# The first units of a fused two-layer kernel's last stage, in another order

## The chip, the cores and the metric

The kernel runs on one core of one Trainium2 chip. A core has TensorE (PE in the profile, with PEld for its weight loads), VectorE (DVE), ScalarE (ACT), GpSimd (POOL) and SyncE (SP), which here only issues transfers. Each engine works through its own instruction stream in order and waits for the others by semaphores. The metric is device time in microseconds (us) of one execution; lower is better.

## The reference, cut to what matters

The input is x, 8 rows of 1024 tokens with 256 features, in float32. Two layers follow each other, each adding a product to x. The last stage of the kernel computes the second one:

```python
xn = _layernorm(x)                                     # first layer
q, k, v = split(xn @ W); q = elu(q) + 1; k = elu(k) + 1
s = (q @ (k.T @ v)) / (q @ k.sum(tokens) + 1e-6)       # per row of x
e = argmax(xn @ gate_w.T)                              # one of 8 experts per token
x = x + s * silu((relu(xn @ wg[e])**2 * (xn @ wu[e])) @ wd[e])
xn = _layernorm(x)                                     # second layer
q, k, v = split(xn @ W_qkv)
scores = where(causal, q @ k.T * scale, -inf)          # in blocks of 128 tokens
p = exp(scores - max(scores)); p = p / (sum(p) + 1e-6)
s = (p @ v) @ W_out.T + b_out
x = x + s * silu(_layernorm(xn) * ln_g + ln_b)
```

The second gate of the reference also has a routed attention, which picks 8 // 16 = 0 tokens for these shapes and so adds nothing.

## The kernel before, in words

The program has three stages: `first_layer`, `experts` and `second_layer`. The tokens are 64 tiles of 128, handled as 32 units of two tiles. `z.res` holds all 64 tiles on the chip, from first to last. At the end of the first layer a tile of `z.res` holds the query rows. They become the attention's values by a product with the key-value matrix of their row of x ("values"). For the last 8 units of that work, `END`, this is done at the beginning of `second_layer`. TensorE multiplies (`whole_values`, L189), VectorE inverts the row sums (`invert_sums`, L195 and L197), and ScalarE scales into `z.res` (`scale_values`, L203). Two bank pairs, `s2_ps` and `pa_ps`, take turns, so `values(p)` waits until ScalarE has emptied its pair of two products ago.

Also there, TensorE folds the second layer's weights (`fold(0)` makes the query-key matrix in `t_ps`, `fold(1)` the value-output matrix in `v_ps`, L1561 and L1566). ScalarE copies the results to `wqk` and `wvo` (L1671). `clear` (L1570) writes constants to banks that later matmuls add to.

The experts' rows were stored to `expert_dram`, sorted by expert. For a unit, GpSimd gathers them with two indirect transfers into one of 4 slots of `four` (L1857). VectorE multiplies the unit's values with them (`scale_rows`, L1695), and x is added. For units 0 to 7 (`DIRECT`) SyncE loads x into a buffer (L1460) and VectorE adds it (`sum_x`, L1701); for the others a GpSimd transfer adds it in `z.res` (`add_x`, L1867). The layer norm then goes through VectorE statistics (L1713, L1723, L1729 to L1731), a GpSimd power and product (`norm_scale`, L1875 and L1877) and a ScalarE apply (`norm_apply`, L1626).

The unit then passes TensorE: `turn` (L1501), `q` (L1488), `v` (L1510), `scores` (L1530), `turn_probs` (L1520) and `attend` (L1541). ScalarE copies and exponentiates in between. VectorE finds the maximum (L1756), prepares the gate (L1737, L1744, L1750), applies it (`gate_rows`, L1778) and adds the rest (`result`, L1784). SyncE stores (L1465).

Each engine runs a `step(n, ...)` for each n. The steps until n = 7 are written out, 8 to 23 are in a loop of eight, and the rest is written out again. In a step the engines handle different units: TensorE has `q(n)` and `turn(n + 1)`, ScalarE has `norm_apply(n + 2)`, VectorE has `result(n - 2)` first, then the statistics of n + 3 between the gate's parts, and `scale_rows(n + 6)` last. GpSimd has `norm_scale(n + 2)`, `add_x(n + 5)` and `gather(n + 8)`; `add_x` and what follows it wait for `scale_rows(n + 5)`.

At the beginning of the stage, TensorE's order is values of END[0], fold 0, fold 1, values of END[1], then the six others, then three clears. VectorE puts `step(-6)` (scale, sum and norm of unit 0) behind the inversions of END[3] and `step(-5)` (unit 1) behind those of END[5]. GpSimd gathers units 0, 1 and 2 before it computes the norm scale of unit 0.

## Time and profile before

| what | us |
| --- | --- |
| median of 3 runs without a profile | 550.27 (549.64 to 550.29) |
| the profiled execution, whole | 555.51 |
| its span, first to last instruction | 553.9 |
| TensorE busy in the span | 508.8 (92%) |
| VectorE busy | 453.5 (82%) |
| ScalarE busy | 391.8 (71%) |
| GpSimd busy | 323.4 (58%) |
| mean granted TensorE clock | 0.987 of full |

The rows are from the one profiled execution, whose whole time is 5.24 us above the median of the runs without a profile. Times in the rows are microseconds from the start of its span. The last stage begins near 328 us and ends with the span. Busy shares are averages over three stages with different limits, so the stage itself has to be read.

### The profile page before, as it was taken

The page shows a single profiled execution, that of the slowest core. Times are in us where ns is not written, and L with a number is a line of the kernel's source. Part 1 is how long each engine was busy: PE and PEld are TensorE (multiplying, and loading weights), DVE is VectorE, ACT ScalarE, POOL GpSimd, SP SyncE. Part 2 cuts the span into 40 slices and gives each one's busy share as a digit, 9 for nine tenths or more (in the row PEclk, how much of TensorE's full clock was granted, in tenths as well). Part 3 has the DMA queues.
Part 4 walks back from the last instruction along what each step waited for, and adds up shares of the span by engine and source line. Part 5 has one row for each costly group of instructions (what it writes and reads, how often), then busy time and mean ns, then how long its engine had stood idle before and what let it go on. Part 6 is the DMA issues. An engine that isn't in the chain of part 4 may idle for free.

```text
span 553.9 us, 12747 instructions
## 1 busy us (share of the span) xinstructions
PE 508.8 (92%) x3554; PEld 468.5 (85%) x3555; DVE 453.5 (82%) x1467; ACT 391.8 (71%) x891; POOL 323.4 (58%) x403
## 2 busy tenths in 40 slices
PE   1899999999999898698899998889999999999995
PEld 0899999999999897498899987668888888888884
DVE  4698888899977665558878774799999999999985
ACT  3687777778777853366677764567888888888884
POOL 4458887878767646222122105876888888787400
PEclk9999999999999999899999999899999999999998
DMA  8833233232311004546677746134655665565311
GB/s 230 219 94 115 83 109 107 85 103 86 105 49 40 30 31 142 125 113 192 196 242 224 228 138 207 57 110 91 139 140 115 128 138 134 114 135 131 78 59 57
DMA packets 59548, 68.07 MB, mean 123 GB/s; under 512 B 11880, under 2 KB 53744, under 8 KB 59504
## 3 DMA queue, kind: packets, MB, share of 16 engines
q1 hardware_dynamic: 45104, 39.73, 23.9%
q0 software_dynamic: 14400, 27.80, 20.8%
q8 instruction: 21, 0.34, 0.3%
q14 instruction: 23, 0.19, 0.1%
HBM read 40.25 MB, written 27.26 MB: 122 GB/s over the span
## 4 chain that ended last, share of the span: by engine, by line
PE 36%; DVE 32%; issue 14%; POOL 7%; ACT 6%; DMA 2%; DVEq 1%; another core or an unknown queue 1%; POOLq 0%; SPq 0%; ACTq 0%
PE gu_ps L1109 5%; PE v_ps L1510 4%; PE q_ps L1488 4%; PE t_ps L1085 3%; PE y_ps L1128 3%; DVE res L696 2%; DVE stats L661 2%; POOL four L1857 2%; POOL rstd L1875 2%; PE s_ps L1530 2%; DVE kf L702 2%; DVE k L708 2%; DVE xt L689 2%; DVE zg L1737 2%; DVE att L1778 1%
## 5 line engine op out<-in xcount | busy, mean ns | idle before, releaser
L1857 POOL DMA_INDIRECT four<-expert_rows,gather_u x64 | 68.7, 1073 | 41.4 <-DMA expert_rows<-y 23.0
L950 POOL DMA_INDIRECT sorted_rows<-xn,row_u x64 | 65.0, 1016 | 15.4 <-issue 14.2
L1488 PE MATMUL q_ps<-xt,wqk 128*128 128x256 f32 x256 | 63.0, 390 | 0.8 <-ACT xt L1606 0.8
L934 POOL TENSOR_TENSOR xn<-xn 128x512 fp32r<-128x512 f32 x32 | 42.9, 1341 | 33.0 <-ACT xn L551 32.9
L1510 PE MATMUL v_ps<-wvo,xt 128*128 128x256 f32 x256 | 60.6, 379 | 0.0
L209 POOL DMA_DIRECT2D four<-sorted_rows x36 | 19.4, 540 | 67.9 <-issue 39.9
L1488 PEld LDWEIGHTS q_ps<-xt,wqk 128*128 128x128 f32 x256 | 50.3, 197 | 8.2 <-ACT xt L1606 1.0
L1875 POOL TENSOR_TENSOR rstd<-var_eps,neg_half 128x4 f32<-128x4 f32 x32 | 38.5, 1202 | 21.0 <-DVE var_eps L1731 10.3
L1510 PEld LDWEIGHTS v_ps<-wvo,xt 128*128 128x128 f32 x256 | 46.3, 190 | 5.0
L1626 ACT ACTIVATE xn2nd<-res,shift,rstd 128x256 f32<-128x256 f32 (+1 forms) x64 | 34.8, 594 | 8.6 <-POOL shift L1877 8.3
L579 ACT ACTIVATE k<-kf 128x512 fp32r<-128x512 f32 x32 | 20.2, 632 | 29.0 <-DVE kf L702 26.9
L1109 PE MATMUL gu_ps<-wgu,xgt 128*128 x288 | 40.0, 282 | 0.0
L166 PE MATMUL tq_ps<-xt,wq 128*128 128x256 f32 x128 | 38.9, 304 | 0.2 <-DVE res L696 0.2
L541 ACT ACTIVATE xn<-four,shift,rstd 128x255 f32<-128x255 f32 x64 | 34.8, 597 | 6.0 <-POOL shift L928 5.9
L166 PE MATMUL m_ps<-k,xn 128*128 128x256 f32 x128 | 36.6, 286 | 2.4 <-DVE k L708 2.4
L166 PE MATMUL k_ps<-wkg,xt 128*128 128x264 f32 x128 | 37.9, 296 | 0.0
L167 PE MATMUL k_ps<-wkg,xt 128*128 128x264 f32 x128 | 37.0, 289 | 0.0
L168 PE MATMUL k_ps<-wkg,xt 128*128 128x264 f32 x128 | 36.8, 287 | 0.0
L167 PE MATMUL tq_ps<-xt,wq 128*128 128x256 f32 x128 | 36.3, 283 | 0.0
L168 PE MATMUL tq_ps<-xt,wq 128*128 128x256 f32 x128 | 36.2, 283 | 0.0
L1109 PEld LDWEIGHTS gu_ps<-wgu,xgt 128*128 128x128 f32 x288 | 35.0, 191 | 1.2
L168 PE MATMUL m_ps<-k,xn 128*128 128x256 f32 x128 | 36.0, 282 | 0.0
(254 smaller groups left out, 1783.2 us busy)
## 6 DMA issues: line engine op xcount, KB each, us to landing
expert_rows<-y SPq DMA_DIRECT2D x36, 256.0 KB, 2.9
four<-in_L_attn_x SPq DMA_DIRECT2D x32, 256.0 KB
out_rows<-att SPq DMA_DIRECT2D x32, 256.0 KB, 2.3
res<-in_L_attn_x POOLq DMA_DIRECT2D x24, 256.0 KB
four<-sorted_rows SPq DMA_DIRECT2D x36, 128.0 KB, 2.4
four<-sorted_rows POOLq DMA_DIRECT2D x36, 128.0 KB, 2.8
wdn<-in_L_ffn_wd SPq DMA_DIRECT2D x2, 512.0 KB, 7.0
sorted_rows<-res SPq DMA_DIRECT2D x8, 128.0 KB, 5.6
```

The lines of the kernel that those rows point to most:

```text
L166: nc.tensor.matmul(out, lhs[0], rhs[0], start=first, stop=False, **kw)
L167: nc.tensor.matmul(out, lhs[0], rhs[1], start=False, stop=False, **kw)
L168: return nc.tensor.matmul(out, lhs[1], rhs[0], start=False, stop=last, **kw)
L541: m = nc.scalar.activation(xn[:, i, t, 0:D - 1], xa[:, i % X_SLOTS, t, 0:D - 1], ACT.Identity, bias=shift[:, i % X_SLOTS, t:t + 1], scale= ...
L934: nc.gpsimd.tensor_tensor(xn2[:, s, 1], xn[:, i], xn2[:, s, 0].bitcast(F32), ALU.subtract).then_inc(g["xn_split"], 1)
L950: nc.gpsimd.indirect_dma_start(out=z.sorted_dram.ap(), out_offset=bass.IndirectOffsetOnAxis(ap=row_u[:, i // CU, k:k + 1], axis=0), in_=xn ...
L1109: m = nc.tensor.matmul(gu_ps[:, i % 2, u * 2 * DE:(u + 1) * 2 * DE], xgt[:, i, k, u, :], z.wgu[:, k, bass.ds(e[u], 1), :].rearrange("p a f ...
L1488: m = nc.tensor.matmul(q_ps[:, j, :], wqk[:, k, j * P:(j + 1) * P], xt[:, i % 2, k, :], start=(j == 0 and k == 0), stop=(k == KD - 1), ski ...
L1510: m = nc.tensor.matmul(v_ps[:, t, :], xt[:, i % 2, k, t * P:(t + 1) * P], wvo[:, k, :], start=(t == 0 and k == 0), stop=(k == KD - 1), ski ...
L1626: m = nc.scalar.activation(xn[:, i % SLOTS, t, :].unsqueeze(1), one_tile(n, t), ACT.Identity, bias=shift[:, i % SLOTS, t:t + 1], scale=rst ...
L1857: nc.gpsimd.indirect_dma_start(out=moe[:, i % SLOTS, t, :], out_offset=None, in_=z.expert_dram.ap(), in_offset=bass.IndirectOffsetOnAxis(a ...
L1875: nc.gpsimd.tensor_tensor(rstd[:, i % SLOTS], var_eps[:, i % SLOTS], z.neg_half[:, 0:2 * UT].rearrange("p (a t) -> p a t", a=2), ALU.pow). ...
```

## The change

TensorE computes the values of END[0] to END[6] in a row. Then comes fold 0, then the values of END[7], and fold 1 last. The clears of `s2_ps` go ahead of the ones for `t_ps`. ScalarE follows: rows of END[0] to END[6], the copy of fold 0, the norm apply of unit 0, rows of END[7], the copy of fold 1.

VectorE handles the unit n + 3 in step n for the first eight units, scale, sum and norm together, where it had unit n + 6. Later units are scaled five ahead (`scale_rows(n + 5)`) where it was six, and the statistics, the moments and the small norm operations of unit n + 3 move behind `gate_rows`. The step of unit 0 is now behind the inversions of END[4], that of unit 1 behind END[6].

GpSimd gathers units 0 and 1 and then alternates: norm scale of 0, gather 2, norm scale of 1, gather 3, norm scale of 2, gather 4, norm scale of 3, gather 5, norm scale of 4, gathers 6 and 7, norm scale of 5, gathers 8 and 9. From step 4 on it has `add_x(n + 4)` and `gather(n + 6)`, where it had n + 5 and n + 8.

```diff
@@ tensor
             values(END[0])
+            pe.wait_ge(z.moe_sems["silu_ready"], z.SLOTS // 2)
+            for p in END[1:-1]:
+                values(p)
             fold(0, t_ps)
+            values(END[-1])
             pe.wait_ge(z.moe_sems["hid_ready"], z.SLOTS // 2)
             fold(1, v_ps)
             clear(a_one[:].rearrange("p t d -> p (t d)"))
-            pe.wait_ge(z.moe_sems["silu_ready"], z.SLOTS // 2)
-            values(END[1])
+            pe.wait_ge(z.rows_ready, UT * (UNITS - 1))
+            for o in (s2_ps[:, 0], s2_ps[:, 1]):
+                clear(o)
...
-            for p in END[2:]:
-                values(p)
+            pe.wait_ge(z.rows_ready, UT * UNITS)
+            clear(pa_ps[:, 1]).then_inc(g["banks_cleared"], 1)
             pe.wait_ge(g["folded_copied"], 2)
-            pe.wait_ge(z.rows_ready, UT * UNITS)
-
-            for o in (s2_ps[:, 0], s2_ps[:, 1], pa_ps[:, 1]):
-                m = clear(o)
-            m.then_inc(g["banks_cleared"], 1)
             run(pe, -1, step, UNITS)
@@ scalar
-            rows(END[0])
+            for p in END[:-1]:
+                rows(p)
             copy_folded(0, wqk, t_ps)
+            step(-2, TURN - 2, 0)
+            rows(END[-1])
             copy_folded(1, wvo, v_ps)
-            for p in END[1:6]:
-                rows(p)
-            step(-2, TURN - 2, 0)
-            for p in END[6:]:
-                rows(p)
@@ vector, in step
+                direct = isinstance(n, int) and n + 3 < DIRECT
                 result(n - 2, at(i, -2))
...
                 centre_gate(*next_one)
                 gate(*back)
                 base_divisor(*back)
                 scale_gate(*next_one)
+                if direct:
+                    scale_rows(*ahead)
                 maximum(n, i)
                 invert_divisor(*back)
                 gate_rows(*back)
...
+                if direct:
+                    sum_x(*ahead)
+                if isinstance(n, int) and n == DIRECT - 4:
+                    scale_rows(n + 4, at(i, 4))
+                x1_complete(*ahead)
+                if there(n + 8, TURN):
+                    index(n + 8, at(i, 8))
+                norm_stats(*ahead)
+                stats_complete(*ahead)
+                if not isinstance(n, int) or n + 5 > DIRECT:
+                    scale_rows(n + 5, at(i, 5))
+                find_moments(*ahead)
+                prepare_norm(*ahead)
@@ vector, start
-            divisors(END[0])
...
+            for p in END[:5]:
+                divisors(p)
+            step(-3, TURN - 3, 0)
             divisors(END[5])
-            step(-5, TURN - 5, 0)
             divisors(END[6])
+            step(-2, TURN - 2, 0)
             divisors(END[7])
-            run(dve, -4, step, UNITS + 1)
+            run(dve, -1, step, UNITS + 1)
@@ gpsimd
+            def load_rows(n):
+                rows_free(n, n % TURN)
+                gather(n, n % TURN)
+
+            def begin(n):
+
+                norm_scale(n + 2, n + 2)
+                if n < 2:
+                    load_rows(n + 4)
+                else:
+                    load_rows(2 * n + 2)
+                    load_rows(2 * n + 3)
+
             def step(n, i, _):
...
+                if isinstance(n, int) and n < SLOTS:
+                    begin(n)
+                    return
+                index_known(n + 6)
+                if isinstance(n, int) and n == SLOTS:
                     norm_scale(n + 2, at(i, 2))
-                if not direct:
-                    add_x(n + 5, at(i, 5))
-                gather(n + 8, at(i, 8))
+                    rows_scaled(n + 4, at(i, 4))
+                else:
+                    rows_scaled(n + 4, at(i, 4))
+                    norm_scale(n + 2, at(i, 2))
+                add_x(n + 4, at(i, 4))
+                gather(n + 6, at(i, 6))
...
-            run(pool, -8, step, UNITS - 3)
+            load_rows(0)
+            load_rows(1)
+            run(pool, -2, step, UNITS - 3)
```

## Rows read from the trace of the kernel before

**Rows 1.** The page: busy time of each engine; the last chain by engine

```profile
PE 508.8 (92%) x3554; PEld 468.5 (85%) x3555; DVE 453.5 (82%) x1467; ACT 391.8 (71%) x891; POOL 323.4 (58%) x403
...
PE 36%; DVE 32%; issue 14%; POOL 7%; ACT 6%; DMA 2%; DVEq 1%; another core or an unknown queue 1%; POOLq 0%; SPq 0%; ACTq 0%
```

**Rows 2.** Timeline of PE from 318 us: start, duration, what, idle before

```profile
328.58 1.91 PE L189 MATMUL s_ps<-kvf,res 128*128 128x258 f32 x8
330.33 1.89 PE L1561 MATMUL t_ps<-wdn 128*128 128x256 f32 x8
...
334.43 1.91 PE L189 MATMUL pa_ps<-kvf,res 128*128 128x258 f32 x8
...
344.90 1.98 PE L189 MATMUL s_ps<-kvf,res 128*128 128x258 f32 x8 [1.42 <-ACT res L203]
...
350.69 0.60 PE L1501 MATMUL t_ps<-ident,xn2nd 128*128 128x128 f32 x4
352.06 3.62 PE L1488 MATMUL q_ps<-xt,wqk 128*128 128x256 f32 x8 [0.77 <-ACT xt L1606]
```

**Rows 3.** Timeline of DVE from 318 us

```profile
330.53 0.16 DVE L195 TENSOR_SCALAR zsum<-s_ps 128x2 f32<-128x2 f32 x1 [0.43 <-PE s_ps L189]
...
340.79 0.69 DVE L1695 TENSOR_TENSOR res<-four,res 128x512 f32<-128x512 f32 x1 [0.39 <-DMA four<-expert_rows,gather_u]
...
343.46 0.16 DVE L1731 TENSOR_SCALAR var_eps<-moments 128x2 f32<-128x2 f32 x1
...
358.50 0.72 DVE L1695 TENSOR_TENSOR res<-four,res 128x512 f32<-128x512 f32 x1 [0.95 <-DMA four<-expert_rows,gather_u]
```

**Rows 4.** Timeline of DVE from 380 us: two `result` operations, one step apart

```profile
388.63 0.68 DVE L1784 TENSOR_TENSOR att<-att,res 128x512 f32<-128x512 f32 x1
...
394.60 0.69 DVE L1784 TENSOR_TENSOR att<-att,res 128x512 f32<-128x512 f32 x1
```

**Rows 5.** Timeline of ACT from 318 us

```profile
330.93 0.84 ACT L203 ACTIVATE res<-s_ps,zinv 128x256 f32<-128x256 f32 x2 [1.54 <-DVE zinv L197]
...
370.03 0.60 ACT L1598 ACTIVATE qt<-q_ps 128x512 f32<-128x512 f32 x1 [3.54 <-remote]
```

**Rows 6.** Timeline of POOL from 310 us

```profile
335.40 0.97 POOL L1857 DMA_INDIRECT four<-expert_rows,gather_u  x1 [0.30 <-issue]
...
343.77 1.04 POOL L1875 TENSOR_TENSOR rstd<-var_eps,neg_half 128x4 f32<-128x4 f32 x1 [2.39 <-DVE var_eps L1731]
344.90 0.60 POOL L1877 TENSOR_TENSOR shift<-neg_mean,rstd 128x2 f32<-128x2 f32 x1
...
355.77 0.96 POOL L1857 DMA_INDIRECT four<-expert_rows,gather_u  x1 [0.30 <-issue]
...
378.01 1.32 POOL L1867 DMA_DIRECT2D res<-in_L_attn_x  x1
```

**Rows 7.** Timeline of SP's queue from 326 us: x loads of units 4 to 7

```profile
334.41 2.52 SPq L1460 DMA_DIRECT2D wdn<-in_L_attn_x  x4
```

**Rows 8.** Windows: span, busy times, granted PE clock, DMA share, GB/s

```profile
352.06:355.48 3.42, 3.42 (x8) 2.75 (x9) 3.25 (x11) 1.23 (x3) 3.15 (x4) 0.51 0.22 67
```

**Rows 9.** Timeline of POOL from 376 us: norm scales and a gather

```profile
394.91 1.28 POOL L1875 TENSOR_TENSOR rstd<-var_eps,neg_half 128x4 f32<-128x4 f32 x1 [0.30 <-issue]
...
418.34 1.51 POOL L1857 DMA_INDIRECT four<-expert_rows,gather_u  x1 [0.31 <-issue]
...
498.52 1.31 POOL L1875 TENSOR_TENSOR rstd<-var_eps,neg_half 128x4 f32<-128x4 f32 x1
```

**Rows 10.** Timeline of PE from 472 us and from 424 us

```profile
483.44 0.66 PE L1501 MATMUL t_ps<-ident,xn2nd 128*128 128x128 f32 x4 [0.57 <-ACT xn2nd L1626]
...
535.00 1.89 PE L1488 MATMUL q_ps<-xt,wqk 128*128 128x256 f32 x8
...
540.87 1.89 PE L1488 MATMUL q_ps<-xt,wqk 128*128 128x256 f32 x8
```

**Rows 11.** DMA issues from 325 to 400 us: size, us to landing

```profile
out_rows<-att SPq DMA_DIRECT2D x5, 256.0 KB, 2.2
```

More of the change, by code:

```diff
@@ L1395, in second_layer @@
     SLOTS, TURN = 4, 8
-    DIRECT, NORMED = 2 * SLOTS, SLOTS
+    DIRECT = 2 * SLOTS
     MOE_SPACE = 3648
@@ L1784, in result @@
                     nc.vector.tensor_tensor(att[:, i % SLOTS], att[:, i % SLOTS], tiles(n), ALU.add).then_inc(g["out_ready"], 1)
-            def first_rows(n, i):
-                scale_rows(n, i)
-                sum_x(n, i)
-            def first_norm(n, i):
-                x1_complete(n, i)
-                norm_stats(n, i)
-                stats_complete(n, i)
-                find_moments(n, i)
-                prepare_norm(n, i)
             def step(n, i, _):
                 back, next_one, ahead = (n - 1, at(i, -1)), (n + 1, at(i, 1)), (n + 3, at(i, 3))
-                normed = isinstance(n, int) and n + 3 < NORMED
+                direct = isinstance(n, int) and n + 3 < DIRECT
                 result(n - 2, at(i, -2))
-                if not normed:
-                    x1_complete(*ahead)
-                if there(n + 9, TURN):
-                    index(n + 9, at(i, 9))
-                if not normed:
-                    norm_stats(*ahead)
-                    stats_complete(*ahead)
                 centre_gate(*next_one)
-                if not normed:
-                    find_moments(*ahead)
                 gate(*back)
-                if not normed:
-                    prepare_norm(*ahead)
                 base_divisor(*back)
                 scale_gate(*next_one)
+                if direct:
+                    scale_rows(*ahead)
                 maximum(n, i)
@@ L1823, in step, with index_known, rows_free @@
                     dve.wait_ge(z.rows_ready, UT * UNITS)
[L1824 to L1829 removed]
+                if direct:
[11 more added lines that the diff above has]
+                prepare_norm(*ahead)
             def divisors(p):
                 invert_sums(nc, dve, z, p, value_banks(p))
[L1834 to L1839 removed]
+            for p in END[:5]:
+                divisors(p)
+            step(-3, TURN - 3, 0)
             divisors(END[5])
[L1841 removed]
             divisors(END[6])
+            step(-2, TURN - 2, 0)
             divisors(END[7])
[L1844 removed]
+            run(dve, -1, step, UNITS + 1)
         def gpsimd(pool):
[L1847 removed]
+            def index_known(n):
                 if there(n):
                     pool.wait_ge(z.index_ready, n + 1)
[L1851 to L1852 removed]
+            def rows_free(n, i):
+                index_known(n)
+                if there(n, SLOTS):
+                    pool.wait_ge(g["moe_scaled"], n - SLOTS + 1)
             def gather(n, i):
```

23 lines of the change are left out of this document (removed).

## The prediction

> **What bounds the kernel now.** The page comes first [rows 1]. TensorE is busy for 92% of the span, VectorE for 82%, and the chain that ended last is shared between them, 36% and 32%. So neither can be dropped as a bound, and the stage has to be read by its timelines.
>
> The first timeline is TensorE's at the beginning of the stage [rows 2]. END[0] starts at 328.58 and the next product 1.75 us later. END[1] starts only at 334.43, since the two folds stand between, and a later product waited 1.42 us for ScalarE to empty its banks. The first `turn` is at 350.69 and q(0) at 352.06, and q(0) took 3.62 us where the later ones take 1.89 [rows 10]. A window around it [rows 8] has a granted clock of 0.51, which is the 1.2 GHz level. TensorE had waited before it.
>
> VectorE's timeline [rows 3] shows why the products waited. Unit 0's scaling started at 340.79, after a wait for the gather. Its norm ended at 343.46 + 0.16 = 343.62, so the whole of scale, sum and norm takes 2.83 us, and inversions of later products stand behind it. GpSimd [rows 6] had issued that gather by 335.40 + 0.97 = 336.37. From there to 340.79 are 4.4 us. A gather later, issued by 355.77 + 0.96 = 356.73, was there at 358.50: 1.8 us. What differs is SyncE's four x loads of 256 KB each [rows 7, 11], issued from 334.41 to 336.93.
>
> The next thing to see is the pace. VectorE's `result` operations are 394.60 - 388.63 = 5.97 us apart [rows 4]. TensorE's q products are 540.87 - 535.00 = 5.87 us apart when nothing holds them [rows 10]. GpSimd's norm scales are (498.52 - 394.91) / 17 = 6.09 us apart on average [rows 9]. The wait of a `turn` at 483.44 for ScalarE's norm apply [rows 10] says that TensorE has run into the slower pair by then. I therefore take the middle of the stage as set by the chain VectorE to GpSimd to ScalarE to TensorE, and the last eight steps or so, with no gathers left, by TensorE. A start that only TensorE makes earlier is worth little; what counts is when GpSimd reaches the norm scale of a unit in the steady part, unit 8 say, now at 394.91.
>
> **The change: products in a row.** One product takes 1.75 us. From its start to `zsum` are 330.53 - 328.58 = 1.95 us, and its rows end 330.93 + 0.84 - 328.58 = 3.19 us after its start [rows 2, 3, 5]. Two products are 3.50 us, so bank pairs come free in time. END[1] starts at 330.33 and END[6] at 330.33 + 5 x 1.75 = 339.1. Then fold 0 is 340.8 to 342.6. END[7] wants the rows of END[5], which now stand behind unit 0's norm on VectorE.
>
> Folding later keeps SyncE's loads of units 4 to 7 back to about 346.5, when fold 1 is done. So gather 0 should land 1.8 us after 336.37, at 338.2, where it was 340.8; that is the one cost I take from a single nearer row, and both ends stay in the range. VectorE is done with END[4]'s sums at 337.9. Unit 0 takes it from 338.3 to 341.1, END[5] and END[6] to 341.6, and the rows of END[5] are scaled by 342.4. END[7] runs from 342.6 to 344.3, fold 1 with the bias product to 346.5, the clears and the ones product, 1.0 us in all, to 347.4. Unit 1 takes VectorE to 344.5, END[7]'s sums to 344.9. ScalarE has rows of END[7] out by 345.8 and the fold's copy by 347.3. So `turn(0)` goes from 350.69 to 347.45, 3.2 us earlier, and q(0) to 348.8.
>
> **The change: scales between gathers.** A norm scale with its product takes GpSimd from 343.77 to 345.50, 1.73 us, and a unit's two gathers 2.5 us [rows 6]. Gather 2 now waits behind the norm scale of unit 0: 343.1 to 345.7, landed 347.5. In the kernel before it was issued by 341.4. VectorE, done with unit 0's gate at 346.5, waits 1.0 us for it and has unit 2 normed at 350.3. Gather 3 is issued by 350.0 and lands at 351.8, or up to 352.8 beside the moved x loads, and the scaling of unit 3 is done by 352.6 to 353.5. The maximum of unit 0 needs scores at 353.7 anyway, so up to 1 us of that delay costs nothing. With the maximum (0.4), the sum (0.7) and the norm (1.5) step 0 ends on VectorE at 356.3, and step 1, one of 6.3, at 362.6. Gathers 4 and 5 are in time, at 356.4 and 362.5.
>
> **The change: three ahead.** The steps of VectorE for units below 8 hold `sum_x` besides the 5.97 us: 6.65. Steps 2 and 3 end at 369.25 and 375.9. Step 4 has two scalings more (units 8 and 9, 0.67 us each) and ends at 383.9, step 5, again one of about 6, at 390.0. The scaling of unit 8 is done 6.1 us into step 4, at 382.0. GpSimd has been waiting for it since 377.9, when the norm scale of unit 6 was done. It issues the add of x (1.32 us [rows 6]) and gather 10 (2.5 with 0.3 ahead) and comes to the norm scale of unit 7 at 386.3, and of unit 8 one full step later, at 392.1. Before, that was 394.91 [rows 9]: 2.8 us are gained in the place that counts. TensorE is well ahead there (q(1) at 353.6, 5.9 us a step, q(6) at 383.3), and will wait some 4 us at `turn(7)`. That may bring the slow clock once more (1.7 us, as in the 3.42 us window at half clock [rows 8]). It can be absorbed: at 5.87 against 6.09 TensorE regains 0.22 a step, 3 us by step 22.
>
> Gathers are now issued two steps later relative to their use. GpSimd ends the issue of a unit's gather about 3 us before VectorE wants it; landing takes 1.8, so this is covered with 1 us to spare. The add of x has 5 us cover, and a store of the same 256 KB landed in 2.2 [rows 11]. Work in all is the same on every engine. GpSimd's full steps reach to n = 25 instead of 23, so TensorE gets free two steps later: 2 x (6.0 - 5.87) = 0.3 us lost. Behind that everything is as before.
>
> **The sum.** -2.8 + 0.3 = -2.5 us on GpSimd's chain. A little of what VectorE gains beyond it (its step 6 starts at 390.0, 394.60 before, 4.6 us) may come through where GpSimd falls less behind; I take 0.2. That is -2.7 us on a profiled 555.51, which gives 552.8 and a span of 551.2. The median of the runs shown is 550.27, 5.24 below the profiled execution. I subtract the same from it: 547.6.
>
> **A rule against this change.** GpSimd operations of one kind vary with their neighbours: a gather took 0.97 us in one row and 1.51 in another [rows 6, 9]. The Trainium skill (SBUF — State Buffer, reading the diagram of its two sides) calls the port pair that GpSimd and VectorE share an "exclusive lock", which VectorE operations with two SBUF inputs can hold against a GpSimd operation that reads SBUF. The trace agrees so far as it has that spread; by the rule GpSimd's step would change with VectorE's order, and by the rows alone it would stay at 6.0 to 6.1. This is the skill's side of the slower rival below.
>
> **The rivals.** *Slower by contention.* GpSimd's step is already as long as VectorE's. If the new order makes it meet longer VectorE operations, each full step stretches. The spread of one gather is 0.54 us; half of it, 0.27 in each of 20 steps, is 5.4 us, and 547.6 + 5.4 = 553.0. It decides from 0.14 us a step. Against it: the phase between the two engines wandered in the trace before and the pace stayed near 6.0. 10%.
>
> *ScalarE's stop.* ScalarE stood still for 3.54 us ahead of the q copy at 370.03, released by nothing that the trace knows [rows 5]. Before, VectorE had buffered work for that time. With units three ahead it does not: the stop would fall at the copy of q(2), 361.3, and hold the maximum and `gate_rows` by 1.65 us, and 1.7 more if the clock falls. The sum becomes -1.0 to +0.6: 549.2 to 550.9. For it: the number of instructions ahead of that copy is the same after the change. Against it: it happened once in the stage, and the runs without a profile are 5 us shorter, so it may be of the profile alone. 15%. The Trainium skill (Runtime: NRT & Kernel Launch, instruction fetch mechanics) has code refilled in blocks of 16 KiB, at a cost "mostly hidden"; no row here shows that the stop is such a refill.
>
> *The change does nothing.* Gather 0 still lands at 340.8, because the stores and first x loads hold it and not the moved ones. Unit 0 is then 2.5 us later, END[7] too, and q(0) at 351.1; 2.7 - 2.4 = 0.3 us remain: 550.0. 11%.
>
> *More than forecast.* GpSimd catches up with VectorE, and 4.6 - 0.3 = 4.3 us arrive: 546.0. 12%.
>
> **How the numbers follow.** The forecast, 547.6 with 546.4 to 549.3 as its own range, has 52%. 0.2% is 1.1 us, about what a measurement of this kernel can tell from no change. Faster, below 549.2: 51 of the forecast, 12 of the last rival, 3 of the stop, in all 66%. Within 1.1 us: 1 of the forecast, 11 from no effect, 10 of the stop, 22%. Slower, above 551.4: 10 of the contention and 2 of the stop where the slow clock delays VectorE in the next step too, 12%. The range is 545.9 to 550.9, down to the full gain and up to the stop with its slow clock. It leaves out the contention and the rest of the stop.
>
> **What would show it.** In the profile after: SyncE's second four loads near 346.5 and not 334.4; unit 0's scaling near 338.3; no wait over 0.5 us between the products END[0] to END[7]; `turn(0)` near 347.45; a wait of about 1 us on VectorE for gather 2; a GpSimd wait of some 4 us for the scaling of unit 8; norm scale of unit 8 near 392.1; norm scales 6.0 to 6.1 apart after it; the `turn` at which TensorE stops waiting two steps later. The prediction fails if GpSimd's steps grow over 6.2, if VectorE waits for gathers in the loop, or if the middle of the stage was not GpSimd's and VectorE's, in which case up to the 3.2 us of q(0) may come or none.

## The result and the profile after

The changed kernel is slower: 552.8 us, median of 20 runs (551.32 to 554.43), against 550.25 for the kernel before in the same series. The ratio is 1.0045, with an interval of 1.0033 to 1.0057. The forecast was 547.6, with a range that ended at 550.9. The profiled execution took 554.43 us with a span of 552.8.

The beginning of the stage is as forecast. This is TensorE's timeline of the changed kernel, for [rows 2]:

```profile
324.38 1.91 PE L189 MATMUL s_ps<-kvf,res 128*128 128x258 f32 x8
326.12 1.91 PE L189 MATMUL pa_ps<-kvf,res 128*128 128x258 f32 x8
...
336.58 1.89 PE L1561 MATMUL t_ps<-wdn 128*128 128x256 f32 x8
338.31 1.91 PE L189 MATMUL pa_ps<-kvf,res 128*128 128x258 f32 x8
340.05 1.89 PE L1561 MATMUL v_ps<-wdn 128*128 128x256 f32 x8
...
343.19 0.60 PE L1501 MATMUL t_ps<-ident,xn2nd 128*128 128x128 f32 x4
344.56 1.99 PE L1488 MATMUL q_ps<-xt,wqk 128*128 128x256 f32 x8 [0.77 <-ACT xt L1606]
...
385.65 0.98 PE L1501 MATMUL t_ps<-ident,xn2nd 128*128 128x128 f32 x4 [3.49 <-ACT xn2nd L1626]
```

The products follow at 1.74 us without a wait, and q(0) starts 344.56 - 324.38 = 20.2 us after END[0], where it was 352.06 - 328.58 = 23.5 [rows 2]. That is 3.3 us; 3.2 were forecast. (The earlier stages ended 4.2 us sooner in this execution, so all that follows counts from the start of END[0].) The last row is the wait at `turn(7)`, 3.49 us where "some 4" stood.

VectorE and GpSimd in the same stretch, for [rows 3, 6]:

```profile
333.57 0.67 DVE L1693 TENSOR_TENSOR res<-four,res 128x512 f32<-128x512 f32 x1
...
342.49 0.69 DVE L1693 TENSOR_TENSOR res<-four,res 128x512 f32<-128x512 f32 x1 [0.30 <-DMA four<-expert_rows,gather_u]
...
348.55 0.69 DVE L1693 TENSOR_TENSOR res<-four,res 128x512 f32<-128x512 f32 x1 [1.66 <-DMA four<-expert_rows,gather_u]
```

```profile
378.62 1.33 POOL L1850 DMA_DIRECT2D res<-in_L_attn_x  x1 [3.77 <-DVE res L1693]
...
388.42 1.08 POOL L1858 TENSOR_TENSOR rstd<-var_eps,neg_half 128x4 f32<-128x4 f32 x1
```

Unit 0's scaling waits for no gather any more, unit 2 waits 0.30 us, unit 3 1.66. GpSimd waits 3.77 us for the scaling of unit 8, and its norm scale of unit 8 starts 388.42 - 324.38 = 64.0 us after END[0], where it was 394.91 - 328.58 = 66.3 [rows 2, 9].

The table gives the start of some q products, in us after END[0], from TensorE's timelines. Its last two rows are kernels of the experiments below: the kernel before with the new beginning alone, and the kernel before with half of the gathers.

```
kernel                     q(0)   q(8)   q(16)   q(31)
before                     23.5   75.9   122.9   212.3
changed                    20.2   73.0   122.1   215.4
changed, again             20.2   71.7   120.5   213.8
new beginning alone        20.2   69.4   118.3   208.4
before, half the gathers   23.1   72.3   120.6   210.0
```

From q(8) to q(31) the kernel before took 136.4 us and the changed one 142.4. The 136.4 flatter the kernel before: its profile has ScalarE's stop [rows 5] ahead of q(8), so q(8) is late, and TensorE then ran at its own pace until q(16), 5.87 us a step. The third and the fourth row were measured side by side, in one set. Against the new beginning alone the changed kernel is 2.3 us behind at q(8) and 5.4 at q(31). So what the beginning gains is mostly gone by q(8) already, and the middle loses 3.1 us more.

A great part of the cause can be read in one step of VectorE's timeline. First the changed kernel, in the loop:

```profile
442.91 0.16 DVE L1687 CAST gather_u<-place 128x2 uint32 x1
442.97 0.74 DVE L1711 BATCH_NORM_STATS2 stats<-res 128x6 f32 x2
443.87 0.69 DVE L1693 TENSOR_TENSOR res<-four,res 128x512 f32 x1 [0.15 <-DVE stats L1711]
444.48 0.24 DVE L1721 BATCH_NORM_AGGREGATE moments<-stats 128x2 f32<-128x6 f32 x2
444.75 0.17 DVE L1727 TENSOR_SCALAR neg_mean<-moments 128x2 f32<-128x2 f32 x1
...
444.97 0.68 DVE L1782 TENSOR_TENSOR att<-att,res 128x512 f32<-128x512 f32 x1
445.57 0.87 DVE L1735 SCALAR_TENSOR_TENSOR zg<-res,neg_mean,lng_half 128x256 f32<-128x256 f32 x2
```

Then the kernel before, in its loop:

```profile
449.42 0.74 DVE L1713 BATCH_NORM_STATS2 stats<-res 128x6 f32 x2
450.20 0.88 DVE L1737 SCALAR_TENSOR_TENSOR zg<-res,neg_mean,lng_half 128x256 f32<-128x256 f32 x2
450.99 0.24 DVE L1723 BATCH_NORM_AGGREGATE moments<-stats 128x2 f32<-128x6 f32 x2
451.15 0.66 DVE L1750 SCALAR_TENSOR_TENSOR zg<-th,zg 128x512 f32<-128x512 f32 x1
451.73 0.16 DVE L1729 TENSOR_SCALAR neg_mean<-moments 128x2 f32<-128x2 f32 x1
```

And the changed kernel once more, in a step that is written out:

```profile
506.47 0.74 DVE L1711 BATCH_NORM_STATS2 stats<-res 128x6 f32<-128x256 f32 x2
507.25 0.69 DVE L1693 TENSOR_TENSOR res<-four,res 128x512 f32<-128x512 f32 x1
507.86 0.24 DVE L1721 BATCH_NORM_AGGREGATE moments<-stats 128x2 f32<-128x6 f32 x2
508.13 0.17 DVE L1727 TENSOR_SCALAR neg_mean<-moments 128x2 f32<-128x2 f32 x1
```

Two places are longer.

**The moments.** An operation that waits for nothing starts before the one ahead has ended: 445.57 is 0.08 before 444.97 + 0.68. `neg_mean` needs `moments`, which now stand directly ahead, and starts 0.03 after their end, 0.27 after their start. In the kernel before a piece of the gate stands between; the next operation follows the moments after 0.16, and by the time of `neg_mean` they are long done. That is 0.11 us more between the two starts, and the steps that are written out, where nothing else grew, are longer by 0.16.

**The statistics.** The wait for them stands ahead of `scale_rows` now. In the written-out step it costs nothing new, 507.25 - 506.47 = 0.78 as before. In the loop it is 443.87 - 442.97 = 0.90, and 0.89 to 1.03 over the eight steps of one turn of the loop, 7.54 in sum; in the kernel before six of the eight are 0.78 and two 0.90 and 0.99, 6.55 in sum. What is different there shows in the chain that ended last in a window around the next step, where VectorE's sequencer (DVEq) has pieces of its own between the statistics and the scaling:

```profile
449.31 0.67 DVE stats L1711 x2
450.00 0.05 DVEq L1692
450.05 0.05 issue
450.10 0.07 DVEq L1693
450.21 0.69 DVE res L1693
```

L1692 is the wait for the gathered rows, whose target is computed in a register in the loop and is a constant in written-out steps. The computation stands behind the wait for the statistics, and the timeline shows nothing that runs over it. That is (7.54 - 6.55) / 8 = 0.12 us a step on average.

VectorE's steps in the loop are mostly 6.24 to 6.35 us, against 5.97, and 6.06 against 5.90 where they are written out. From 410 to 500 us the mean is 6.33 against 6.01. (Two steps in the middle of the loop are longer than that, 6.89 and 6.44 where the kernel before has 6.30 and 6.08; no run took that part apart.) GpSimd stands idle for VectorE almost nowhere, as the waits of the changed kernel from 400 to 530 us show (engine, line, what it waited for: total, times, longest):

```profile
ACT xn2nd L1626 <- POOL shift L1860: 24.2, 21, 1.7
...
POOL rstd L1858 <- DVE var_eps L1729: 5.6, 3, 2.9
...
DVE res L1693 <- DVE stats L1711: 2.9, 14, 0.3
```

Its own operations have changed as well. The groups by line from 410 to 500 us (count, busy us, mean ns), changed and then before:

```profile
L1858 POOL TENSOR_TENSOR rstd<-var_eps,neg_half 128x4 f32<-128x4 f32 x14 | 17.5, 1248 | 0.3 <-DVE var_eps L1729 0.3
L1860 POOL TENSOR_TENSOR shift<-neg_mean,rstd 128x2 f32<-128x2 f32 x14 | 6.1, 433 | 1.1
```

```profile
L1875 POOL TENSOR_TENSOR rstd<-var_eps,neg_half 128x4 f32<-128x4 f32 x15 | 17.3, 1151 | 0.0
L1877 POOL TENSOR_TENSOR shift<-neg_mean,rstd 128x2 f32<-128x2 f32 x15 | 4.1, 277 | 1.2
```

So two theories stood after the first profile. *The order*: VectorE's step is longer by its own two waits. *GpSimd*: the order of VectorE's operations stretches GpSimd's, and GpSimd sets the pace.

### The profile page after: what moved, and what is told of

The parts are those of the page before. It is cut to its first block, busy times and chain, and to the rows that moved or that the text cites. A ratio compares the mean times of both kernels' runs of the same rounds, so it can differ in the third digit from the quotient of the medians.

```text
span 552.8 us, 12716 instructions
## 1 busy us (share of the span) xinstructions
PE 509.3 (92%) x3554; PEld 464.7 (84%) x3555; DVE 458.3 (83%) x1466; ACT 391.0 (71%) x891; POOL 333.2 (60%) x403
## 4 chain that ended last, share of the span: by engine, by line
DVE 41%; PE 37%; issue 11%; ACT 6%; POOL 2%; DVEq 2%; DMA 1%; SPq 0%; ACTq 0%; POOLq 0%
PE gu_ps L1109 5%; PE v_ps L1510 3%; PE t_ps L1085 3%; PE y_ps L1128 3%; DVE res L696 3%; DVE zg L1735 3%; PE q_ps L1488 3%; DVE stats L661 3%; DVE stats L1711 2%; DVE res L1693 2%; DVE xt L689 2%; DVE zg L1748 2%; DVE kf L702 2%; DVE zg L1742 2%; DVE k L708 2%
## 5 line engine op out<-in xcount | busy, mean ns | idle before, releaser
L1840 POOL DMA_INDIRECT four<-expert_rows,gather_u x64 | 72.1, 1126 | 41.9 <-DMA expert_rows<-y 22.3
L950 POOL DMA_INDIRECT sorted_rows<-xn,row_u x64 | 66.6, 1041 | 15.4 <-issue 13.7
L1510 PE MATMUL v_ps<-wvo,xt 128*128 128x256 f32 x256 | 62.0, 386 | 0.0
L1488 PE MATMUL q_ps<-xt,wqk 128*128 128x256 f32 x256 | 60.6, 380 | 0.8 <-ACT xt L1606 0.8
L1488 PEld LDWEIGHTS q_ps<-xt,wqk 128*128 128x128 f32 x256 | 48.6, 190 | 7.3 <-ACT xt L1606 1.0
L1510 PEld LDWEIGHTS v_ps<-wvo,xt 128*128 128x128 f32 x256 | 47.5, 195 | 5.3
L579 ACT ACTIVATE k<-kf 128x512 fp32r<-128x512 f32 x32 | 20.2, 633 | 30.8 <-DVE kf L702 30.8
L166 PE MATMUL m_ps<-k,xn 128*128 128x256 f32 x128 | 36.8, 287 | 3.3 <-DVE k L708 3.3
L1850 POOL DMA_DIRECT2D res<-in_L_attn_x x24 | 32.0, 1334 | 9.0 <-issue 5.1
```

The lines of the kernel that those rows point to most:

```text
L166: nc.tensor.matmul(out, lhs[0], rhs[0], start=first, stop=False, **kw)
L950: nc.gpsimd.indirect_dma_start(out=z.sorted_dram.ap(), out_offset=bass.IndirectOffsetOnAxis(ap=row_u[:, i // CU, k:k + 1], axis=0), in_=xn ...
L1488: m = nc.tensor.matmul(q_ps[:, j, :], wqk[:, k, j * P:(j + 1) * P], xt[:, i % 2, k, :], start=(j == 0 and k == 0), stop=(k == KD - 1), ski ...
L1510: m = nc.tensor.matmul(v_ps[:, t, :], xt[:, i % 2, k, t * P:(t + 1) * P], wvo[:, k, :], start=(t == 0 and k == 0), stop=(k == KD - 1), ski ...
L1840: nc.gpsimd.indirect_dma_start(out=moe[:, i % SLOTS, t, :], out_offset=None, in_=z.expert_dram.ap(), in_offset=bass.IndirectOffsetOnAxis(a ...
```

## The experiments

Kernels of one set ran on one chip, one after the other. From set to set the time of the kernel before differs, so it stands with each. A kernel marked "one run" has one time and no interval. Steps are from one `gate_rows` or statistics operation of VectorE to the next; a mean step is that of the `gate_rows` from 410 to 500 us.

### Set 1 (before: 550.33 us)

**start_alone**: the kernel before with the new beginning only. TensorE and ScalarE have the changed order, VectorE's units 0 and 1 stand behind END[4] and END[6]. VectorE stays six ahead, GpSimd eight.

```diff
             values(END[0])
+            for p in END[1:-1]:
+                values(p)
             fold(0, t_ps)
+            values(END[-1])
...
-            divisors(END[4])
+            step(-6, TURN - 6, 0)
             divisors(END[5])
-            step(-5, TURN - 5, 0)
             divisors(END[6])
+            step(-5, TURN - 5, 0)
```

> The kernel before with only the new beginning: the products END[0] to END[6] in a row, fold 0, END[7], fold 1, on TensorE and ScalarE, and VectorE's unit 0 behind END[4] and unit 1 behind END[6]. VectorE's and GpSimd's later order stay as before (six and eight ahead). Theory A (the loss is VectorE's longer step, from the new order of the steady part): q(0) comes 3.3 us earlier relative to END[0] as in the changed kernel, VectorE's step stays at 5.97 us and the time is 1 to 3.5 us below the kernel before. Theory B (the loss comes from the start, TensorE too early, long waits in the direct units): it is as slow as the changed kernel, +1 to +3 us.

547.62 us, ratio 0.9952 (0.9932 to 0.9972). q(0) is at +20.2, VectorE's step is 5.97, q(31) at +208.2. GpSimd's norm scale of unit 8 is at +62.2, where the kernel before has it at +66.3 and the changed one at +64.0. So the whole loss lies in the rest of the change, and the new beginning by itself is worth the 2.7 us forecast for the whole, and 3.05 in set 3.

**moments_in_a_row**: the kernel before, with the small norm operations directly behind the moments.

```diff
                     find_moments(*ahead)
+                    prepare_norm(*ahead)
                 gate(*back)
-                if not normed:
-                    prepare_norm(*ahead)
                 base_divisor(*back)
```

> The kernel before with the small norm operations directly behind the moments they read; before, the gate's 0.58 us stood between. Nothing else moves. Theory A: each step of VectorE grows by the exposed wait, 0.12 to 0.2 us, times some 20 steps in which VectorE counts: +2 to +4 us. Theory C: GpSimd gets the variance 0.6 us earlier and nothing is lost, 0 or below.

553.69 us, 1.0054 (1.0036 to 1.0072). VectorE's step is 6.12. Its timeline has `moments` at 442.18 and `neg_mean` at 442.46, 0.28 later. One uncovered wait in the otherwise unchanged kernel costs 3.4 us; 23 steps of 0.15 are 3.5.

**spread_tail**: the changed kernel with both waits covered. `result(n - 1)` stands between the statistics and `scale_rows`, the small norm operations behind the next `centre_gate`.

```diff
-                result(n - 2, at(i, -2))
                 centre_gate(*next_one)
+                if not (isinstance(n, int) and n + 2 < DIRECT):
+                    prepare_norm(n + 2, at(i, 2))
...
                 norm_stats(*ahead)
+                result(n - 1, at(i, -1))
                 stats_complete(*ahead)
...
                 find_moments(*ahead)
-                prepare_norm(*ahead)
+                if direct:
+                    prepare_norm(*ahead)
```

> The changed kernel with the end of VectorE's step spread again: result(n - 1) between the statistics of unit n + 3 and scale_rows(n + 5), and the small norm operations behind the next step's centre_gate for units from 8 on. Same instructions in all, same number of units ahead. Theory A (the 0.28 us by which VectorE's step grew are the exposed waits for its own results, statistics and moments): the step falls from 6.25 to 5.97 and the time by 4 to 6 us, to 547 to 549. Theory C (GpSimd's saturated step, stretched by contention for the shared memory port, sets 6.25): the step stays at 6.2 or more and the time within 1 us of the changed kernel, 552 to 554.

553.85 us, 1.006 (1.0037 to 1.0082). A miss for the theory of the order alone. VectorE has steps of 5.90 to 5.99 where nothing holds it, but the mean is 6.43, and it waits for others. These are the waits of spread_tail from 400 to 530 us:

```profile
ACT xn2nd L1626 <- POOL shift L1863: 26.5, 21, 1.9
...
POOL res L1853 <- issue: 9.1, 16, 1.2
POOL rstd L1861 <- DVE var_eps L1729: 5.7, 3, 3.2
PE t_ps L1501 <- ACT xn2nd L1626: 4.6, 11, 0.7
DVE att L1776 <- PE pa_ps L1541: 4.3, 8, 0.8
```

VectorE waits for TensorE, TensorE for the norm apply, and that for GpSimd, whose gathers take 1266 ns on average instead of 1125 in the kernel before and 1132 in the changed one. With VectorE relieved, GpSimd is the limit.

**half_gather** (one run): the changed kernel with one gather instead of two for each unit from 8 on. Half of the expert rows of those units are left out.

```diff
-                    dve.wait_ge(moe_loaded[i % SLOTS], turns(n, i, 16 * UT) + (SCATTERED + 16 * UT))
...
+                        dve.wait_ge(moe_loaded[i % SLOTS], turns(n, i, 16) + (SCATTERED + 48))
...
-                    for t in range(UT):
+                    for t in range(UT if isinstance(n, int) and n < DIRECT else 1):
```

> The changed kernel with one gather instead of two for each unit from 8 on; it leaves out half of those units' expert rows. GpSimd's step falls by 1.3 us to about 5. Theory A (VectorE's own length): VectorE's step stays at 6.2 to 6.3 us. Theory C (GpSimd sets the pace): the step falls to 5.9, TensorE's own pace.

552.12 us, and VectorE's step stays mostly at 6.24 to 6.27, its mean at 6.32. GpSimd now waits for VectorE in every step, as the waits from 400 to 500 us show:

```profile
POOL rstd L1861 <- DVE var_eps L1732: 23.8, 16, 2.4
```

So GpSimd is not what makes 6.24 of 5.97 here. Both theories hold a part: VectorE's order sets 6.24, and GpSimd stands close behind it.

### Set 2 (before: 555.47 us)

**cover_moments**: the changed kernel, `result(n - 1)` moved between the moments and what reads them.

```diff
-                result(n - 2, at(i, -2))
...
                 find_moments(*ahead)
+                result(n - 1, at(i, -1))
                 prepare_norm(*ahead)
```

> The changed kernel with result(n - 1) between the moments and the small norm operations, nothing else moved (result stood right behind them). Theory A (exposed waits on VectorE): the wait for the moments is hidden, VectorE's loop step falls by 0.12 to 0.16 us, from 6.25 to 6.1, and 20 steps give 2 to 3 us: 549.5 to 551. Theory D (with VectorE relieved, GpSimd's stretched step or the shorter way round from unit n + 3 takes its place, as in the spread kernel): no gain, 552 to 554.

557.35 us, 1.0033 (1.0015 to 1.0052). Many steps are 6.08 to 6.12, but others 6.6 to 7.1, and the mean is 6.32, where the changed kernel has 6.33. The step is shorter where VectorE sets it; the time follows little, if at all, since the changed kernel's own ratio is 1.0045.

**scale_behind_stats**: the kernel before, `scale_rows(n + 6)` moved from the end of the step to right behind the wait for the statistics.

```diff
                     stats_complete(*ahead)
+                if not isinstance(n, int) or n > 2:
+                    scale_rows(n + 6, at(i, 6))
                 centre_gate(*next_one)
...
-                else:
+                elif isinstance(n, int) and n <= 2:
                     scale_rows(n + 6, at(i, 6))
```

> The kernel before with scale_rows(n + 6) of the steps from 3 on moved from the end of VectorE's step to right behind the statistics of unit n + 3. In the loop its wait needs a register computation. Theory A, second part (that computation is exposed behind the wait for the statistics): VectorE's step grows by 0.12 to 0.22 us in the loop and not in the written-out steps, 16 x 0.15 = 2.4 us: 552 to 553.5. If the place does not matter: 550.3 within 0.5.

559.9 us, 1.0082 (1.0056 to 1.0109), 4.4 us more where 1.7 to 3.2 were expected. The step in the loop is 6.21 at least and 6.32 on average, with the statistics at 440.99 and the scaling at 441.88, 0.89 later as in the changed kernel. But the written-out steps grew too, from 5.97 to 6.12, which was not expected, and there the register computation has no part. This is the end of such a step:

```profile
389.15 0.88 DVE L1778 SCALAR_TENSOR_TENSOR att<-pa_ps,inv,zg 128x256 f32<-128x256 f32 x2
390.06 0.69 DVE L1784 TENSOR_TENSOR att<-att,res 128x512 f32<-128x512 f32 x1
```

`result` now stands directly behind `gate_rows`, whose output it reads, and starts 0.91 after it. In the kernel before the scaling stood between them and started 0.79 after `gate_rows`. So the edit uncovered one more wait, which the changed kernel doesn't have: about half of the loop's growth is that wait and about half the register computation (0.89 against 0.78). The 4.4 us are the price of both and not of the register computation alone.

**start_between**: start_alone, and GpSimd's scales between its gathers, six ahead kept.

```diff
+                if isinstance(n, int) and -6 <= n < 0:
+                    if n > -6 and first:
+                        norm_scale(n + 5, at(i, 5))
+                        rows_free(n + 7, at(i, 7))
+                        gather(n + 7, at(i, 7))
+                    if n == -1:
+                        for m in (6, 7):
+                            rows_free(m, m)
+                            gather(m, m)
+                    return
```

> The new beginning alone, with the changed kernel's GpSimd order for it: norm scale 0 before gather 2, norm scale 1 before gather 3 and so on. VectorE's order stays six ahead. If putting the scales between the gathers costs what the prediction said (about 1 us of waiting on VectorE for gather 2, partly hidden), the time is 0 to 1 us above the 547.6 of the beginning alone; if it is a main part of the loss, 2 us or more above.

558.93 us, 1.0072 (1.0044 to 1.01), with q(2) at +40.6 where start_alone has +33.5. TensorE stood still for 7.65 us once, and in this set's profiles ScalarE had such stops as in [rows 5], so it was run again in set 3.

**spread_half** (one run): spread_tail with one gather per unit from 8 on; half of those units' expert rows are left out.

> The spread kernel with one gather instead of two for each unit from 8 on; it leaves out half of those units' expert rows. Theory A with D (VectorE's own step is 5.95 once its waits are covered, and GpSimd's step of 6.3 took its place): VectorE's step is 5.9 to 6.0, and the time 4 us or more below the 552.1 that the changed kernel had with one gather. If the short way round through the engines holds it instead, the step stays at 6.2 or more.

550.03 us against 555.47. VectorE's step is mostly 5.84 to 5.87 and 5.89 on average, and so is TensorE's from q(8) to q(24), where 5.87 is the pace that TensorE has by itself [rows 10]. With both waits covered and GpSimd relieved the changed order is about as fast as TensorE allows.

### Set 3 (before: 549.85 us)

**start_again**, **between_again** and **changed_again** are start_alone, start_between and the changed kernel, together in one set.

> The new beginning alone once more, beside the two below on one chip, since the second set of runs had another time for the kernel before (555.5 us) than the first (550.3). If its gain is the chip's alone, it falls within 0.5 us of the kernel before; if it is the order's, it is again 2 to 3.5 us below it.

546.8 us, 0.9943 (0.9922 to 0.9964). So the gain is the order's.

> The new beginning with the scales between the gathers once more. In its profile TensorE stood still for 7.65 us ahead of a transpose without a cause in the trace, and VectorE waited 7.5 us for gathers in all. Theory E (the gathers come too late with this order, 7.5 us of waits): 3 us or more above start_again. Theory F (stops of that chip, not the order): within 1.5 us of start_again, with no such stop in the profile.

552.49 us, 1.0044 (1.0025 to 1.0064). VectorE's step is 5.97, so the steady part is untouched, but q(31) is at +213.8 against +208.4. The waits of between_again from 330 to 400 us show where the 5.4 us are:

```profile
PE pa_ps L1520 <- ACT pr L1639: 8.1, 1, 8.1
DVE res L1693 <- DMA four<-expert_rows,gather_u: 7.9, 4, 3.0
...
ACT pr L1639 <- DVE ntop L1754: 4.9, 1, 4.9
```

GpSimd issues the gathers later, and VectorE, which scales six units ahead, wants them early. It stands waiting for rows that nobody needs yet, and the maximum of unit 0 is queued behind that.

> The changed kernel itself, on the same chip as the two above. Theory A: 4 to 6 us above start_again, the sum of 20 longer VectorE steps (0.28 us each), whatever the chip.

553.16 us, 1.0051 (1.003 to 1.0072), 6.4 us above start_again. It waits 1.7 us for gathers, and q(2) is at +31.0, where start_again has +33.7. So with three ahead the scales between the gathers cost little there. But q(7) is at +65.5 against +63.5: in between VectorE's steps are 6.4 to 7.3 us, as they hold the sums with x and the uncovered moments, and `turn(7)` waits 2.50 us for the norm apply. In start_again TensorE's steps are 5.95 there, without such a wait.

**before_half** (one run): the kernel before with one gather per unit from 8 on, half of those units' expert rows left out.

> The kernel before with one gather instead of two for each unit from 8 on; it leaves out half of those units' expert rows. If VectorE's own length sets the middle of the stage there, VectorE's step stays at 5.97 us and the time within 1 us of the kernel before; if GpSimd does, the step falls to 5.87 and the time by 2 us.

547.61 us, 2.2 below the set's median and 0.7 below the lowest of its 27 runs; within 1 us was expected if VectorE alone set the pace, and it is one run. VectorE's step is 5.97, unchanged. GpSimd's changes: its norm scales of units 8 to 25 are 6.03 us apart, where they are 6.09 in the kernel before and 6.10 in start_again, and it now waits for VectorE in every step from 410 to 500 us:

```profile
POOL rstd L1878 <- DVE res L1698: 17.2, 15, 1.3
```

In start_again over the same stretch it does so once, and each norm scale starts further behind VectorE's variance, 3.0 us at unit 8 and 4.3 at unit 25. So in the kernel before GpSimd's own 6.09 is the slower one, and VectorE, 6.02 on average over the same units, stands right behind it.

### Set 4 (before: 548.08 us, one run)

Still open was how the 0.28 us split, since cover_moments had not turned its part into time. Both kernels are one run and have one gather per unit from 8 on, leaving out half of those units' expert rows, so that GpSimd is out of the way; half_gather is what they are compared with, by the q products, as it ran in another set.

**cover_moments_half** is cover_moments so relieved.

> The changed kernel with one gather per unit from unit 8 on (half of those units' expert rows are left out, as in half_gather), and with result(n-1) put between the moments of a unit and the small norm operations that read them. half_gather had VectorE steps of 6.24 to 6.27 us and took 552.1 us. If the uncovered wait for its own moments is one part of the lost 0.28 us a step, VectorE's step falls to 6.10 to 6.14 and the time by 19 steps of 0.14, to 549 to 550. If the step is set by GpSimd or by reads that collide, it stays at 6.24 or more and the time at 552.

**scale_first_half** puts the register computation ahead of the statistics and `result(n - 1)` behind their wait. The wait for the moments stays uncovered.

```diff
+                scale_rows(n + 5, at(i, 5))
                 norm_stats(*ahead)
                 stats_complete(*ahead)
-                scale_rows(n + 5, at(i, 5))
+                result(n - 1, at(i, -1))
                 find_moments(*ahead)
                 prepare_norm(*ahead)
```

> The changed kernel with one gather per unit from unit 8 on (half of those units' expert rows are left out), and with scale_rows ahead of norm_stats again and result(n-1) between the wait for the statistics and the moments. Then the register computation of the loop stands behind no late wait, while the wait of the small norm operations for the moments stays uncovered. If the register computation is the other part of the lost 0.28 us, the loop step falls from 6.24 to about 6.12 and the time to 549 to 550. If it is nothing, the step stays at 6.24 and the time at 552.

```
kernel               step in the loop   q(8)   q(31)   one run
half_gather          6.24 to 6.27       71.8   214.1   552.12
cover_moments_half   6.08 to 6.11       69.8   208.9   546.99
scale_first_half     6.11 to 6.12       70.4   211.2   549.61
```

Each step fell by about the size expected: 0.16 for the moments and 0.13 for the register computation. The mean steps are 6.32, 6.13 and 6.18. From q(8) to q(31) half_gather took 142.3 us, the first 139.1 and the second 140.8. The times are lower than half_gather's by 5.1 and 2.5 us in a set where the kernel before is 2.2 us faster; the q products, which the earlier stages don't touch, by 5.2 and 2.9, of which 2.1 and 1.5 are there at q(8) already. So the uncovered moments cost in the first units too. How much of what the changed kernel has lost by q(8) they are isn't settled: in cover_moments, with whole gathers, q(8) is at +71.0 and only 0.7 us earlier than in changed_again. This is scale_first_half's step, for comparison with the one above:

```profile
445.38 0.31 DVE L1687 CAST gather_u<-place 128x2 uint32 x1
445.45 0.68 DVE L1696 TENSOR_TENSOR res<-four,res 128x512 f32 x1
446.05 0.75 DVE L1714 BATCH_NORM_STATS2 stats<-res 128x6 f32 x2
446.83 0.69 DVE L1785 TENSOR_TENSOR att<-att,res 128x512 f32<-128x512 f32 x1
447.44 0.24 DVE L1724 BATCH_NORM_AGGREGATE moments<-stats 128x2 f32<-128x6 f32 x2
447.72 0.17 DVE L1730 TENSOR_SCALAR neg_mean<-moments 128x2 f32<-128x2 f32 x1
```

From the statistics to the next operation it is 0.78 again, in the loop; the register computation stands ahead of the statistics and costs nothing that the timeline shows. From the moments to `neg_mean` it is still 0.28.

## Why the prediction was wrong

**Products in a row** was right: 3.2 us forecast for q(0), 3.3 measured. But the prediction held that "a start that only TensorE makes earlier is worth little", and nearly all of it arrived at the end with no other part of the change (550.33 to 547.62, and 549.85 to 546.8; VectorE's units 0 and 1 had moved with it).

**Gather 0** with SyncE's loads later was right as far as unit 0 waited for nothing; no run varied the loads alone. Its scaling is 333.57 - 324.38 = 9.2 us after END[0]; it was forecast at 338.3 - 328.58 = 9.7.

**Scales between gathers** was right for the changed kernel: a wait of 0.3 for gather 2 where 1.0 was said, and one of 1.66 for gather 3, mostly in the shade of the maximum. What the prediction did not say is what this costs when VectorE is six ahead. It is 5.7 us (between_again against start_again).

**Three ahead** has its numbers right and its cause wrong. GpSimd waited 3.77 us for the scaling of unit 8 ("some 4"), reached its norm scale 2.3 us earlier after END[0] ("2.8 us are gained in the place that counts"; 1.4 in changed_again), and `turn(7)` waited 3.49. But with the new beginning alone, and units six ahead as before, that norm scale is at +62.2 and +62.3 (start_alone, start_again), some 4 us earlier than the +66.3 of the kernel before, or 3 against the +65.2 of before_half, which has no stop of ScalarE ahead of it. So the gain there is the new beginning's, and the rest of the change gave 1.9 to 2.6 us of it back. That the forecast came near is luck: the gain in this place was compared with the old kernel only.

**The step that failed** is "Work in all is the same on every engine", with "Behind that everything is as before". The busy time of VectorE is nearly the same, 458.3 against 453.5 us, but the order inside the step is part of its length. The move puts two results directly ahead of what waits for them: the moments ahead of `neg_mean`, and the statistics' wait ahead of a register computation. The step went from 5.97 to 6.24 and more, 6.33 on average. GpSimd's norm scales of units 8 to 25, forecast "6.0 to 6.1 apart", came 6.35 apart, and 6.21 in changed_again, so the prediction's own sign "if GpSimd's steps grow over 6.2" is met. Measured side by side, changed_again lost 5.4 us to start_again by q(31), 2.3 of them by q(8). (The lead of 2.9 us over the kernel before at q(8) is mostly the stop in that one's profile; before_half has +72.3 there.) The wait for the moments is shown alone both ways: put into the kernel before (moments_in_a_row, 3.4 us) and taken out of the changed one (cover_moments_half, the step 0.16 shorter). The register computation is shown by its removal in scale_first_half (0.13 a step, one run); scale_behind_stats has it together with another wait. The rows for it stood in the trace of before: `neg_mean` starts 0.74 us after the moments, with an operation of the gate between. The prediction counted the work of the moved operations and never asked what had stood between them.

**The pace of the middle** was put down to a chain with GpSimd's 6.09 as its slowest member. That was right for the kernel before, but by a margin of 0.07 us only: with GpSimd relieved, before_half runs at VectorE's 6.03. So whatever lengthened VectorE's step by more than that had to show, and the change added 0.27 and more.

**The rival that came true** is, by its time, the slower one: 553.0 against 552.8. That the two numbers meet is luck, as by its mechanism it is right only in part. It said that GpSimd's steps would stretch by 0.27; they did by 0.26, and by 0.11 in changed_again, but half_gather shows that VectorE's own waits are enough for that. GpSimd comes second: it is why covering VectorE's waits brought nothing in spread_tail and cover_moments (mean steps 6.43 and 6.32, against 5.89 in spread_half and 6.13 in cover_moments_half). So the chance of 12% for slower was too small for a change that rewrites the order of the engine that sets the pace.

**What stretches GpSimd's operations** is open. With the same shapes their lengths change with VectorE's order, and not all one way. In the changed kernel the norm scale went from 1151 to 1248 ns and its product from 277 to 433, with the gathers nearly the same. In spread_tail the gathers went from 1125 to 1266, and the other two fell to 1092 and 195. The Trainium skill (SBUF — State Buffer, reading the diagram) has a port pair that the two engines take from each other for whole instructions; the trace agrees in so far as `scale_rows`, an operation with two SBUF inputs, is among those that were moved. No run varied the ports alone.

**ScalarE's stop** of 3.54 us [rows 5] is in no profile of sets 1, 3 and 4 nor in that of the changed kernel; every profile of set 2 has a stop of 4.8 to 6.2 us in an earlier stage, and two of the four one of 3.6 or 4.2 us at the query copy as well. Apart from the first profile of the kernel before they go with the set and not with the kernel. What they are stays open, and with it part of the comparison of the two first profiles.

The best version found is start_alone, 0.9952 and 0.9943 of the time before: the new beginning without the new steady order.

## What to carry to other kernels

When an operation is moved on an engine that sets the pace, its length is not the only price. Look at which result the next operation reads, and at what stood between them: that operation was the cover of a wait. In a loop, look also for the register computation that a wait's target needs, and keep it ahead of any wait that ends late. And when two engines have steps of 6.0 and 6.1 us, relieve both or expect the second to take what the first gives up: half_gather alone and cover_moments alone brought little or nothing, both together 3.2 us from q(8) to q(31). Last, when a change has several parts, price each against the kernel with the others in it: the beginning alone was the better kernel. An experiment that moves an operation can uncover a wait where it is taken away, too, as scale_behind_stats did.

## What the runs showed of the hardware

In these timelines a VectorE operation that waits for nothing starts about 0.08 us before the end of the one ahead, and one that reads the result directly ahead starts 0.03 after it ended (`neg_mean` behind the moments; `result` behind `gate_rows` in scale_behind_stats). The Trainium skill (VectorE: DVE Perf Modes, The DRAIN you can't avoid) says of a row of copies that a semaphore between them "costs nothing extra". The case here is another one, an operation that would otherwise overlap the one ahead, and for it the wait did cost: 0.15 us a step in moments_in_a_row, 3.4 us in all.

A register computation behind a late wait, with pieces of 0.05 and 0.07 us on the sequencer, lengthened VectorE's loop step by 0.12 us on average. In front of the statistics it costs nothing that the timeline shows (scale_first_half).

The time of one kernel moves between sets: the kernel before took 550.3, 555.5, 549.85 and 548.1 us in the four. Sets 1 and 2 ran on the chip of the same number, so it isn't shown that the chip makes the 5 us; ScalarE's stops, which of the four sets only set 2 has, are of that size. Ratios hold only inside a set; the changed kernel had 1.0045 and 1.0051 in two.
